# Moving the last tile's second shared step behind the sorted steps of a mixture-of-experts round

## The chip, the cores and the metric

The kernel runs on one core of a Trainium2 chip. The time is device microseconds (us) of one execution. A core has five engines with a queue of instructions each: TensorE (PE in the profile, its weight loads PEld), VectorE (DVE), ScalarE (ACT), GpSimd (POOL) and SyncE (SP). SP issues most of the transfers, POOL the indirect ones. Engines wait for one another and for transfers through semaphores, and each takes its own instructions in order.

## The reference

The input has 4096 rows of 256 numbers. Two layers follow each other. What the change touches is the feed-forward part of the first layer:

```python
for j in range(C):                                   # C = 2 rounds
    residual = xf
    gate = (xf @ router_W[j] + router_b[j]) / TEMP
    _, ids = jax.lax.top_k(gate + gate_bias[j], 2)   # two of 6 experts for each row
    weights = softmax over the two chosen gates
    h  = einsum('nh,ehi->eni', xf, exp_Wup) + exp_bup
    h  = silu(h @ exp_Wg + exp_bg) * h
    eo = h @ exp_Wdown + exp_bdown
    combined = einsum('ne,enh->nh', weights, eo)
    s = (xf @ share_Wup + share_bup).reshape(-1, NS, I)     # NS = 2 shared units
    s = silu(s @ share_Wg + share_bg) * s
    y = residual + combined + (s @ share_Wdown + share_bdown).sum(axis=1)
    xf = y * rsqrt(mean(y * y) + EPS) * norm_w[j]
```

Ahead of it stands an attention part (A below), behind it the second layer's attention (C) and its feed-forward part with 8 experts (D).

## The kernel before

The stages run one after another: A, two expert rounds (B0, B1), C, D. In a round the 4096 rows are 8 tiles (`NB`) of 512 rows. A round is a row of 37 steps (`STEPS`), each of which sends 512 rows through one unit:

- 8 steps "new", numbers 0 to 7: the first shared unit, for tile 0 to 7. They keep their product in `shared` and have no down product of their own.
- 8 steps "old", 8 to 15: the second shared unit for the same tiles. The tile's rows come back from memory (`b_rows`) into one of four slots of `got`. The two shared units have the same down weights, so the product is added to the one kept in `shared` (`joined`, L1539), and one down product serves both. Its result is added to the tile in `x` (L1553).
- 21 steps "sort", 16 to 36, here called s0 to s20: blocks of 512 rows that are sorted by expert. POOL gathers the rows of a block with four indirect transfers into a slot of `got` (`gathers`, L1731), and scatters the results from a slot of `sent` with four more (`scatters`, L1738).

The order of work is written out by hand. `turn_steps` goes through j with three steps at a time: now (j), after (j+1) and third (j+2). PE's body for one j is: gate(after), turn(third), up(after), down(now). The turn is the eight transposes of L1202 of the rows of step j+2; it waits for those rows. Gate and up are 12 matmuls of 512 columns each, down is 24 of 256 columns, and four more in a dense step (L1246). DVE's body is: taken(third), gated(after), send(now). Steps whose unit is new (`fresh`) also have their weights split into a high and a low part, by ACT (L1318) and DVE (L1510).

At the same time the routing is made, spread over the steps. The table by which rows are gathered is summed up in four parts at j = 9 to 12 (`INVERT_AT`, L1694) and turned into the indices `b_gather_i` by `index_vector` (L1699 to L1704) at the end of j = 12. PE's turn at j = 13 waits until the last part has been read from its bank.

POOL's order in a round: wait for the indices (`gather_at`), six gathers (`AHEAD`), then for each k the gather of k+6 and the scatter of k. The first four blocks wait until the dense steps have left `got`, which is the turn of step 15 (in the code: `rnd*STEPS + 2*NB - 1`). A scatter waits for its send (`o`).

At the end of round 0, SP waits for all scatters and fetches, for each tile, its two rows of results per token (`fetch_sync`, into `back`), and ACT (L1419), DVE (L1435, L1437, L1482) and POOL combine and normalise them, tile by tile, before PE can turn tile 0 of round 1. At the end of round 1 the same happens with `close_sync`, whose buffers `close_back` and `x_old` belong to stage C.

Of the kernel before, what the change touches and what calls it, by code (L numbers as in the profile page):

```python
# [14 lines left out]
P = 128  # L15
N, D = 4096, 256
KD = D // P
NT = N // P
TB = 512
NB = N // TB  # L20
# [15 lines left out]
SLOT_TOP = PICKS * N  # L36
CLOSE_BUFS = 4
TURN_COLS = 8
BACKS = 3
# [30 lines left out]
NQ, NGD = max(NQB, NQD), -(-NBD // GROUP)  # L70
STEPS, LB, WM = 2 * NB + NBB, 2 + NBB, KD * D
OUTS = STEPS - NB
# [931 lines left out]
class Round:  # L1004
    def __init__(self, rnd):
        self.rnd, self.first, self.count = rnd, rnd * STEPS, STEPS
        order = [("new", t) for t in range(NB)] + [("old", t) for t in range(NB)] + [("sort", k) for k in range(NBB)]
        self.steps, users = [], {}
        for j, (kind, n) in enumerate(order):
            load = {"new": 0, "old": 1}.get(kind, 2 + n)  # L1010
            i = self.first + j
            self.steps.append(Step(i, kind, rnd * (NBB if kind == "sort" else NB) + n, rnd * LB + load, load not in users, users.get(load - 2)))
            users[load] = self.steps[-1]

    def at(self, j):
        return self.steps[j] if 0 <= j < self.count else None


# [25 lines left out]
def b_sync(sp, b, s, r, d, dram, rnd):  # L1044
    q0, t0, expert = rnd * LB, rnd * NB, {0: slice(0, 1), 1: slice(1, 2)}

    def first_mats(n):
        q = q0 + n
        i, _, previous = RAW_TURN[q]
        if previous is not None:  # L1050
            sp.wait_ge(r.wu_lo.sem, r.wu_lo.at(previous))
        if i >= 2 and n < 2 + RAWS:
            sp.wait_ge(r.joined.sem, r.joined.at(rnd * NB + NB - 1))
        if n >= 2:
            expert[n] = bass.ds(sp.value_load(b.expert_i[0:1, n - 2:n - 1], min_val=NS, max_val=U0 - 1), 1)
        sp.dma_start(b.w_raw[i][:, 0:WM], d["units0"][expert[n], :, 0:WM].squeeze(0)).then_inc(r.loaded[i].sem, 16)
        if q < 2:
            sp.wait_ge(r.folded.sem, r.folded.at(q))
            sp.dma_start(b.w_raw[q][:, WM:2 * WM], b.up_turned[:, q, :]).then_inc(r.loaded[i].sem, 16)
        else:  # L1060
            sp.dma_start(b.w_raw[i][:, WM:2 * WM], dram.folded[expert[n], :, :].squeeze(0)).then_inc(r.loaded[i].sem, 16)
# [23 lines left out]
    if rnd == 1:  # L1085
        for i in range(SENDS):
            sp.wait_ge(r.scattered[i].sem, r.scattered[i].at(uses_of(NBB, SENDS, i) - 1))
        for t in range(BACKS):
            fetch_sync(sp, b, r, dram.kept[0], t)
    for t in range(NB):  # L1090
# [8 lines left out]
    if rnd == 0:  # L1099
        sp.wait_ge(r.fold_kept.sem, r.fold_kept.at(0))  # L1100
    for t in range(NB):
        if t >= 4:
# [5 lines left out]
    for n in range(2, LB + 1):  # L1108
        if n < LB:
            first_mats(n)  # L1110
        if n >= 3:
            last_mat(n - 1)
            biases(n - 1)


def first_sort(kg):
    return (kg // NBB) * STEPS + 2 * NB + kg % NBB


def sort_out(kg):  # L1120
    return (kg // NBB) * OUTS + NB + kg % NBB

# [58 lines left out]
def b_tensor(pe, b, s, r, rnd):  # L1181
# [3 lines left out]
    def turn(st):  # L1185
# [3 lines left out]
        elif st.kind == "old":  # L1189
            t = st.n % NB  # L1190
            pe.wait_ge(r.reloaded[t % 4].sem, r.reloaded[t % 4].at(rnd * 2 + t // 4))
            src = lambda c, f: b.got[:, t % 4, c, f * P:(f + 1) * P]
        else:
# [75 lines left out]

    first, rounds = 2 * NB, (NBB - 2) // TURNS  # L1270
    for j, now, after, third in turn_steps(rnd):
# [32 lines left out]
def b_scalar(act, b, s, r, rnd):  # L1304
    B = b.bank

    def rounded(sig, done, st, lo, hi):
# [6 lines left out]
        elif st.before is not None:  # L1314
            act.wait_ge(done.sem, done.at(index(st.before)))
        elif st.load >= 2:
            act.wait_ge(done.sem, done.at(rnd * (OUTS if done is r.down_ps else STEPS) - 1))
        act.activation(b.w_hi_flat[st.load % 2][:, lo:hi], b.w_raw[i][:, lo:hi], ACT.Copy).then_inc(sig.sem, 1)  # L1318
# [390 lines left out]
def b_gpsimd(g, b, s, r, dram, rnd):  # L1709
# [13 lines left out]
    def gathers(k):  # L1723
# [3 lines left out]
        else:  # L1727
            g.wait_ge(r.gT_ps.sem, r.gT_ps.at(rnd * STEPS + 2 * NB - 1))
        for c in range(QB):
# [49 lines left out]
def close_sync(sp, b, s, r, d, dram):  # L1779
# [9 lines left out]

    old_rows(0)  # L1790
    sp.dma_start(b.heads, d["consts"][:, 1, :]).then_inc(s.load_c_small.sem, 16)
    sp.dma_start(b.c_bo, d["bo_rows"]).then_inc(s.load_c_small.sem, 16)
# [799 lines left out]
def program(nc, d, out):  # L2592
    ctx = ExitStack()
    with ctx:
# [110 lines left out]
        with ExitStack() as sc:  # L2705
# [15 lines left out]
            with ExitStack() as over:  # L2721
                b.sent_both = sb(over, "sent", [P, 2, QB, D])
                b.sent = [b.sent_both[:, i, :, :] for i in range(2)]
                b.back = [b.got[:, 2 * i:2 * i + 2, :, :] for i in range(2)] + [b.sent_both]
                b.junk = sb(over, "junk", [P, 2, D])
# [7 lines left out]
        with ExitStack() as sc:  # L2733
            b.close_back, b.x_old = [sb(sc, f"close_back{t}", [P, PICKS, CT, D]) for t in range(CLOSE_BUFS)], [sb(sc, f"x_old{t}", [P, CT, D]) for t in range(CLOSE_BUFS)]
            b.c_raw = {n: sb(sc, n + "_raw", [P, KD, D]) for n in C_MATS}
# [8 lines left out]
            b.c_outT = sb(sc, "c_outT", [P, KD, TB])  # L2744
            b.c_y, b.c_e, b.c_l, b.c_t = (sb(sc, n, [P, 2 * KD, TB]) for n in ("c_y", "c_e", "c_l", "c_t"))
            bC = Names(b)

# [347 lines left out]
```

## Time and profile before

| | us |
|---|---|
| median of 3 runs | 2036.41 |
| lowest and highest | 2035.42, 2038.35 |
| profiled execution, its own time | 2036.51 |
| its span, first to last instruction | 2034.6 |

| engine | busy us | share of the span |
|---|---|---|
| PE | 1766.5 | 87% |
| PEld | 1559.6 | 77% |
| DVE | 1402.5 | 69% |
| ACT | 1029.3 | 51% |
| POOL | 821.1 | 40% |

The mean granted TensorE clock is 0.927. The profiled execution spent 1.9 us outside its span. A share of the span is an average over stages: what a change is worth is read from the stage that it touches. In the span, round 0 begins at about 658 us, round 1 at about 1045 us, and stage C at about 1426 us.

### The profile page before, as it was taken

The page shows a single profiled execution, that of the slowest core. Times are in us where ns is not written, and L with a number is a line of the kernel's source. Part 1 is how long each engine was busy: PE and PEld are TensorE (multiplying, and loading weights), DVE is VectorE, ACT ScalarE, POOL GpSimd, SP SyncE. Part 2 cuts the span into 40 slices and gives each one's busy share as a digit, 9 for nine tenths or more (in the row PEclk, how much of TensorE's full clock was granted, in tenths as well). Part 3 has the DMA queues.
Part 4 walks back from the last instruction along what each step waited for, and adds up shares of the span by engine and source line. Part 5 has one row for each costly group of instructions (what it writes and reads, how often), then busy time and mean ns, then how long its engine had stood idle before and what let it go on. Part 6 is the DMA issues. An engine that isn't in the chain of part 4 may idle for free. (4 is left out here: it accounts for less than half of the span.)

```text
span 2034.6 us, 31786 instructions
## 1 busy us (share of the span) xinstructions
PE 1766.5 (87%) x11154; PEld 1559.6 (77%) x11154; DVE 1402.5 (69%) x2513; ACT 1029.3 (51%) x2078; POOL 821.1 (40%) x868
## 2 busy tenths in 40 slices
PE   5899999999978999999949999996499883899990
PEld 4788888888877878888838788886266683899990
DVE  4665556546433888777756987775798687688886
ACT  4344334434412344555546355553688353788882
POOL 2132232323211114777721157776221030788840
PEclk8899999999998899999969999998699966899995
DMA  4100000000023131666553226664600013688857
GB/s 155 62 1 11 10 10 0 10 10 0 10 88 103 55 105 40 202 192 202 168 190 122 91 78 199 203 186 146 221 32 1 1 63 114 206 278 277 257 193 258
DMA packets 146216, 231.43 MB, mean 114 GB/s; under 512 B 28082, under 2 KB 103092, under 8 KB 141108
## 3 DMA queue, kind: packets, MB, share of 16 engines
q1 hardware_dynamic: 122484, 165.47, 24.6%
q0 software_dynamic: 23616, 64.52, 10.5%
q8 instruction: 60, 0.98, 0.2%
q14 instruction: 56, 0.46, 0.1%
HBM read 174.07 MB, written 55.33 MB: 113 GB/s over the span
## 5 line engine op out<-in xcount | busy, mean ns | idle before, releaser
L178 POOL TENSOR_TENSOR spare_g<-neg_half 128x1 f32<-128x1 f32 x80 | 20.7, 259 | 622.2 <-ACT a_sg L538 142.5
L167 PE MATMUL bank<-gT_hi,w_hi 128*128 128x512 f32 x592 | 246.0, 416 | 2.4 <-DVE gT_lo L1526 2.4
L167 PE MATMUL bank<-gT_hi,w_lo 128*128 128x512 f32 x592 | 237.3, 401 | 0.0
L167 PE MATMUL bank<-gT_lo,w_hi 128*128 128x512 f32 x592 | 236.2, 399 | 0.0
L1731 POOL DMA_INDIRECT got<-b_rows,b_gather_i x168 | 171.9, 1023 | 65.1 <-issue 50.6
L1526 DVE TENSOR_TENSOR gT_lo<-bank,gT_hi 128x512 fp32r<-128x512 f32 x148 | 97.0, 689 | 132.4 <-ACT gT_hi L1334 99.1
L1364 ACT ACTIVATE m_hi<-gs 128x512 fp32r<-128x512 f32 x116 | 73.0, 633 | 128.3 <-DVE gs L1533 69.0
L167 PEld LDWEIGHTS bank<-gT_hi,w_lo 128*128 128x128 f32 x592 | 113.2, 191 | 27.6
L167 PE MATMUL bank<-w_hi,m_hi 128*128 128x256 f32 x464 | 130.5, 281 | 2.8 <-DVE shared L1555 1.4
L167 PEld LDWEIGHTS bank<-gT_hi,w_hi 128*128 128x128 f32 x592 | 113.6, 192 | 22.9 <-DVE gT_lo L1526 2.5
L167 PEld LDWEIGHTS bank<-gT_lo,w_hi 128*128 128x128 f32 x592 | 113.9, 192 | 21.5
L167 PE MATMUL bank<-w_lo,m_hi 128*128 128x256 f32 x464 | 130.4, 281 | 0.0
L167 PE MATMUL bank<-w_hi,m_lo 128*128 128x256 f32 x464 | 130.1, 280 | 0.0
L2390 POOL DMA_INDIRECT d_got<-d_rows,d_gather_i x78 | 95.7, 1227 | 68.8 <-DVE d_gather_i L2321 45.4
L2396 POOL DMA_INDIRECT d_kept<-d_sent,d_scatter_i x78 | 97.6, 1252 | 45.9 <-DVE d_sent L2551 24.6
L884 POOL TENSOR_TENSOR a_aTm<-a_aT,masks 128x512 f32<-128x512 f32 x56 | 71.4, 1286 | 107.2 <-PE bank L416 82.6
L1355 ACT ACTIVATE gs<-bank,w_cols 128x512 f32<-128x512 f32 x84 | 57.7, 690 | 97.3 <-PE bank L167 97.3
L1738 POOL DMA_INDIRECT b_kept<-sent,b_scatter_i x88 | 90.4, 1028 | 26.8 <-issue 26.8
L167 PE MATMUL bank<-d_gT_hi,v_hi 128*128 128x256 f32 x312 | 93.0, 298 | 1.8 <-DVE d_gT_lo L2531 1.8
L577 ACT ACTIVATE a_ax<-bank 128x512 f32<-128x512 f32 x48 | 28.7, 597 | 128.0 <-PE bank L416 128.0
L1334 ACT ACTIVATE gT_hi<-bank 128x512 fp32r<-128x512 f32 x148 | 82.0, 598 | 21.1 <-PE bank L1202 20.9
L167 PE MATMUL bank<-v_hi,d_m_hi 128*128 128x256 f32 x312 | 91.3, 293 | 1.4 <-issue 0.9
(455 smaller groups left out, 5731.2 us busy)
## 6 DMA issues: line engine op xcount, KB each, us to landing
v_raw<-in_units SPq DMA_DIRECT2D x39, 1024.0 KB, 5.0
w_raw<-in_units SPq DMA_DIRECT2D x52, 256.0 KB, 4.9
shared<-in_units SPq DMA_DIRECT2D x40, 256.0 KB, 4.4
b_rows<-x SPq DMA_DIRECT2D x16, 512.0 KB, 2.9
got<-b_rows SPq DMA_DIRECT2D x16, 512.0 KB, 3.9
close_back<-b_kept SPq DMA_DIRECT2D x16, 512.0 KB, 7.8
d_back<-d_kept SPq DMA_DIRECT2D x16, 512.0 KB, 8.5
w_raw<-b_folded SPq DMA_DIRECT2D x24, 256.0 KB
```

What stands on the lines that cost most here:

```text
L167: ins = pe.matmul(out, a, b, start=first and n == 0, stop=last and n == of - 1)
L178: eng.tensor_tensor(b.spare_g[:, i:i + 1], b.neg_half[:, 0:1], b.neg_half[:, 0:1], ALU.mult)
L577: act.activation(b.ax[:, :], B[1][:, :], ACT.Copy).then_inc(s.ax.sem, 1)
L884: g.tensor_tensor(four(b.aTm[l % 2][:, :]), four(b.aT[:, :]), mid(b.maskT[:, l, :], CT), ALU.mult).then_inc((s.aTm if l else s.aTm0).sem, 1)
L1334: act.activation(b.gT_hi[st.par][:, f, :], B[6 + f][:, :], ACT.Copy).then_inc(r.gT_hi.sem, 1)
L1355: act.activation(product_of(b, st)[:, o, :], B[2 + o][:, :], ACT.Silu, bias=b_bias(b, st, 1, o)).then_inc(r.sg.sem, 1)
L1364: act.activation(b.m_hi[st.par][:, o, :], b.gs[:, o, :], ACT.Copy).then_inc(r.m_hi.sem, 1)
L1526: v.tensor_tensor(b.gT_lo[st.par][:, f, :], B[6 + f][:, :], f32(b.gT_hi[st.par][:, f, :]), ALU.subtract).then_inc(r.gT_lo.sem, 1)
L1731: g.indirect_dma_start(b.got[:, kg % 4, c, :], None, dram.rows[rnd], bass.IndirectOffsetOnAxis(b.gather_i[:, q:q + 1], 0)).then_inc(r.gath ...
L1738: g.indirect_dma_start(dram.kept[rnd], bass.IndirectOffsetOnAxis(b.scatter_i[:, q:q + 1], 0), b.sent[kg % SENDS][:, c, :], None).then_inc( ...
L2390: g.indirect_dma_start(b.got[n % 6][:, c, :], None, rows, bass.IndirectOffsetOnAxis(b.gather_i[:, q:q + 1], 0)).then_inc(r.gathered[n % 6] ...
L2396: g.indirect_dma_start(kept, bass.IndirectOffsetOnAxis(b.scatter_i[:, q:q + 1], 0), b.sent[k % 4][:, c, :], None).then_inc(r.scattered[k % ...
```

## The change

One step of each round is moved: the step "old" of tile 7 leaves place 15 and becomes step 36, behind s20. The sorted steps become 15 to 35. With it:

- The order of steps and all indices that count them (`FRONT_STEPS` = 15). The moved step finds its unit's weights gone, so they are loaded once more (`LATE_LOAD`, one more load in each round, `LB` from 23 to 24) and split again by ACT and DVE.
- SP reloads the last tile's rows at the end of the round's loads, into the slot of `got` that s17 leaves (`row_slot`).
- POOL's first four gathers wait for the turn of step 14 instead of step 15.
- The third and fourth weight buffers (which lie in `shared`) wait for the joined product of tile 6 instead of tile 7.
- `back` is laid out anew: the first fetch goes into `sent_both`, the next two into `got`; the third waits for the turn of the round's last step.
- In stage C the buffers `close_back` and `x_old` are placed elsewhere, with a gap (`C_GAP`) between them, so that the first row of returned data does not touch what the moved step still uses; all further loads of that stage wait for the last send (`o`).

Where the routing is made (j = 7 to 15) does not change.

```diff
+LATE = 1
+FRONT_STEPS, LATE_LOAD = 2 * NB - LATE, 2 + NBB
-STEPS, LB, WM = 2 * NB + NBB, 2 + NBB, KD * D
+STEPS, LB, WM = 2 * NB + NBB, 3 + NBB, KD * D
...
-        order = [("new", t) for t in range(NB)] + [("old", t) for t in range(NB)] + [("sort", k) for k in range(NBB)]
+        order = [("new", t) for t in range(NB)] + [("old", t) for t in range(NB - LATE)]
+        order += [("sort", k) for k in range(NBB)] + [("old", t) for t in range(NB - LATE, NB)]
...
-            load = {"new": 0, "old": 1}.get(kind, 2 + n)
+            load = {"new": 0, "old": 1 if j < FRONT_STEPS else LATE_LOAD}.get(kind, 2 + n)
...
+def row_slot(t, rnd):
+    return t % 4 if t < NB - LATE else (rnd * NBB + NBB + t - (NB - LATE)) % 4
...
         for t in range(BACKS):
+            if t == BACKS - 1:
+                sp.wait_ge(r.gT_ps.sem, r.gT_ps.at(STEPS - 1))
             fetch_sync(sp, b, r, dram.kept[0], t)
...
-    for t in range(NB):
+    for t in range(NB - LATE):
         if t >= 4:
             sp.wait_ge(r.gT_ps.sem, r.gT_ps.at(rnd * STEPS + NB + t - 4))
...
+    for t in range(NB - LATE, NB):
+        sp.wait_ge(r.gT_ps.sem, r.gT_ps.at(first_sort(rnd * NBB + NBB - 4 + t - (NB - LATE))))
+        sp.dma_start(b.got[:, row_slot(t, rnd), :, :], rows_of(dram.rows[rnd], t)).then_inc(r.reloaded[t % 4].sem, 16)
...
         if k >= 4:
             g.wait_ge(r.gT_ps.sem, r.gT_ps.at(first_sort(kg - 4)))
         else:
-            g.wait_ge(r.gT_ps.sem, r.gT_ps.at(rnd * STEPS + 2 * NB - 1))
+            g.wait_ge(r.gT_ps.sem, r.gT_ps.at(rnd * STEPS + FRONT_STEPS - 1))
...
     old_rows(0)
+    sp.wait_ge(r.o.sem, r.o.at(2 * OUTS - 1))
     sp.dma_start(b.heads, d["consts"][:, 1, :]).then_inc(s.load_c_small.sem, 16)
...
-                b.back = [b.got[:, 2 * i:2 * i + 2, :, :] for i in range(2)] + [b.sent_both]
+                b.back = [b.sent_both, b.got[:, 2:4, :, :], b.got[:, 0:2, :, :]]
```

## Rows read from the trace of the kernel before

**Rows 1.** Waits, PE: line, released by, us in total, times, longest.
```profile
PE bank L1202 <- DVE x L1482: 25.8, 1, 25.8
PE bank L2048 <- ACT m_hn L1826: 19.0, 1, 19.0
```
**Rows 2.** Windows: length, busy us of PE PEld DVE ACT POOL, clock, DMA share, GB/s.
```profile
830.00:1000.00 170.00, 170.00 (x1022) 149.25 (x1022) 128.88 (x205) 94.19 (x164) 131.01 (x128) 1.00 0.64 193
1024.20:1045.00 20.80, 0.00 (x0) 0.00 (x0) 7.52 (x15) 8.19 (x28) 4.83 (x8) 0.50 0.54 177
1045.00:1054.90 9.90, 8.58 (x32) 7.51 (x33) 5.74 (x12) 4.96 (x15) 1.47 (x3) 0.50 0.94 302
1734.50:1741.00 6.50, 5.46 (x24) 5.06 (x25) 2.89 (x5) 4.33 (x8) 5.09 (x5) 0.50 0.40 103
```
**Rows 3.** Timeline, POOL, both rounds: start, us, instruction, idle before and releaser.
```profile
804.70 1.22 POOL L1731 DMA_INDIRECT got<-b_rows,b_gather_i  x1 [7.30 <-PE bank L1202]
...
809.20 1.09 POOL L1731 DMA_INDIRECT got<-b_rows,b_gather_i  x1 [0.30 <-issue]
...
1023.60 0.97 POOL L1738 DMA_INDIRECT b_kept<-sent,b_scatter_i  x1 [0.30 <-issue]
...
1195.35 1.09 POOL L1731 DMA_INDIRECT got<-b_rows,b_gather_i  x1 [7.21 <-PE bank L1202]
...
1413.06 0.97 POOL L1738 DMA_INDIRECT b_kept<-sent,b_scatter_i  x1 [0.30 <-issue]
```
**Rows 4.** Timeline, PE, first transposes of steps 15 and s0, both rounds.
```profile
802.71 0.33 PE L1202 MATMUL bank<-ident,got 128*128 128x128 f32 x1
...
812.56 0.38 PE L1202 MATMUL bank<-ident,got 128*128 128x128 f32 x2
...
1193.45 0.33 PE L1202 MATMUL bank<-ident,got 128*128 128x128 f32 x1 [0.16 <-DVE b_found L1694]
...
1203.30 0.27 PE L1202 MATMUL bank<-ident,got 128*128 128x128 f32 x1
```
**Rows 5.** Timeline, DVE, last write of the gather indices, both rounds.
```profile
803.25 0.20 DVE L1704 TENSOR_SCALAR b_gather_i<-b_gather_i 128x84 int32<-128x84 int32 x1
...
1193.98 0.20 DVE L1704 TENSOR_SCALAR b_gather_i<-b_gather_i 128x84 int32<-128x84 int32 x1
```
**Rows 6.** Timeline, stage D, its first gathers: DVE, POOL, PE.
```profile
1726.88 0.20 DVE L2321 TENSOR_SCALAR d_gather_i<-d_gather_i 128x78 int32<-128x78 int32 x1
...
1727.91 1.09 POOL L2390 DMA_INDIRECT d_got<-d_rows,d_gather_i  x1 [45.37 <-DVE d_gather_i L2321]
...
1734.55 0.69 PE L2434 MATMUL bank<-ident,d_got 128*128 128x128 f32 x2 [8.60 <-DMA d_got<-d_rows,d_gather_i]
```
**Rows 7.** Timeline, ACT, first product of the turns of s19 and s20.
```profile
991.15 1.08 ACT L1334 ACTIVATE gT_hi<-bank 128x512 fp32r<-128x512 f32 x2
...
1000.46 1.08 ACT L1334 ACTIVATE gT_hi<-bank 128x512 fp32r<-128x512 f32 x2
```
**Rows 8.** Timeline, DVE, products and sends: a dense step, then both rounds' ends.
```profile
806.72 0.75 DVE L1533 SCALAR_TENSOR_TENSOR gs<-bank,bias_cols,gs 128x512 f32<-128x512 f32 x1 [0.64 <-PE bank L167]
...
809.98 1.28 DVE L1553 TENSOR_TENSOR x<-x,bank 128x512 f32<-128x512 f32 x2
...
1012.04 0.75 DVE L1533 SCALAR_TENSOR_TENSOR gs<-bank,w_cols,gs 128x512 f32<-128x512 f32 x1 [0.65 <-PE bank L167]
...
1014.11 0.68 DVE L1510 TENSOR_TENSOR w_lo<-w_raw,w_hi 128x512 fp32r<-128x512 f32 x1
...
1019.26 0.69 DVE L1555 TENSOR_TENSOR sent<-bank,w_b 128x512 f32<-128x512 f32 x1 [0.66 <-PE bank L167]
...
1402.78 0.75 DVE L1533 SCALAR_TENSOR_TENSOR gs<-bank,w_cols,gs 128x512 f32<-128x512 f32 x1 [0.65 <-PE bank L167]
```
**Rows 9.** Timeline, stage D, the last send and its scatter.
```profile
1987.38 0.69 DVE L2551 TENSOR_TENSOR d_sent<-bank,v_b 128x512 f32<-128x512 f32 x1 [2.72 <-PE bank L167]
...
1988.35 0.97 POOL L2396 DMA_INDIRECT d_kept<-d_sent,d_scatter_i  x1 [1.16 <-DVE d_sent L2551]
```

More of the change, by code:

```diff
@@ L37 @@
 CLOSE_BUFS = 4
+C_GAP = 5168
 TURN_COLS = 8
@@ L1044, in b_sync @@
 def b_sync(sp, b, s, r, d, dram, rnd):
-    q0, t0, expert = rnd * LB, rnd * NB, {0: slice(0, 1), 1: slice(1, 2)}
+    q0, t0, expert = rnd * LB, rnd * NB, {0: slice(0, 1), 1: slice(1, 2), LATE_LOAD: slice(1, 2)}
     def first_mats(n):
@@ L1052, in first_mats @@
         if i >= 2 and n < 2 + RAWS:
-            sp.wait_ge(r.joined.sem, r.joined.at(rnd * NB + NB - 1))
-        if n >= 2:
+            sp.wait_ge(r.joined.sem, r.joined.at(rnd * NB + NB - LATE - 1))
+        if 2 <= n < LATE_LOAD:
             expert[n] = bass.ds(sp.value_load(b.expert_i[0:1, n - 2:n - 1], min_val=NS, max_val=U0 - 1), 1)
@@ L1112, in b_sync @@
             last_mat(n - 1)
-            biases(n - 1)
+            if n - 1 < LATE_LOAD:
+                biases(n - 1)
+    for t in range(NB - LATE, NB):
+        sp.wait_ge(r.gT_ps.sem, r.gT_ps.at(first_sort(rnd * NBB + NBB - 4 + t - (NB - LATE))))
+        sp.dma_start(b.got[:, row_slot(t, rnd), :, :], rows_of(dram.rows[rnd], t)).then_inc(r.reloaded[t % 4].sem, 16)
 def first_sort(kg):
-    return (kg // NBB) * STEPS + 2 * NB + kg % NBB
+    return (kg // NBB) * STEPS + FRONT_STEPS + kg % NBB
 def sort_out(kg):
-    return (kg // NBB) * OUTS + NB + kg % NBB
+    return (kg // NBB) * OUTS + NB - LATE + kg % NBB
 def product_of(b, st):
@@ L1191, in turn @@
             pe.wait_ge(r.reloaded[t % 4].sem, r.reloaded[t % 4].at(rnd * 2 + t // 4))
-            src = lambda c, f: b.got[:, t % 4, c, f * P:(f + 1) * P]
+            src = lambda c, f: b.got[:, row_slot(t, rnd), c, f * P:(f + 1) * P]
         else:
@@ L1268, in step @@
         down(now)
-    first, rounds = 2 * NB, (NBB - 2) // TURNS
+    first, rounds = FRONT_STEPS, (NBB - 2) // TURNS
     for j, now, after, third in turn_steps(rnd):
@@ L1316, in rounded @@
         elif st.load >= 2:
-            act.wait_ge(done.sem, done.at(rnd * (OUTS if done is r.down_ps else STEPS) - 1))
+            ended = LATE if st.load % LB == 0 else 0
+            act.wait_ge(done.sem, done.at(rnd * (OUTS if done is r.down_ps else STEPS) - 1 - ended))
         act.activation(b.w_hi_flat[st.load % 2][:, lo:hi], b.w_raw[i][:, lo:hi], ACT.Copy).then_inc(sig.sem, 1)
@@ L2733, in program @@
         with ExitStack() as sc:
-            b.close_back, b.x_old = [sb(sc, f"close_back{t}", [P, PICKS, CT, D]) for t in range(CLOSE_BUFS)], [sb(sc, f"x_old{t}", [P, CT, D]) for t in range(CLOSE_BUFS)]
             b.c_raw = {n: sb(sc, n + "_raw", [P, KD, D]) for n in C_MATS}
@@ L2745, in program @@
             b.c_y, b.c_e, b.c_l, b.c_t = (sb(sc, n, [P, 2 * KD, TB]) for n in ("c_y", "c_e", "c_l", "c_t"))
+            b.x_old = [sb(sc, f"x_old{t}", [P, CT, D]) for t in range(1, CLOSE_BUFS)]
+            b.c_gap = sb(sc, "c_gap", [P, C_GAP])
+            b.x_old.insert(0, sb(sc, "x_old0", [P, CT, D]))
+            b.close_back = [sb(sc, f"close_back{t}", [P, PICKS, CT, D]) for t in range(CLOSE_BUFS)]
             bC = Names(b)
```

## The prediction

> **What bounds the kernel now.** I read the waits of PE first. The two longest stand where a round hands over: PE waits 25.8 us before it can turn tile 0 of round 1, and 19.0 us at the start of stage C [rows 1]. The change puts one step's PE work into such holes, so the question is what releases PE there and whether that comes sooner. What releases it is the chain scatter, landing, fetch, weigh, mix, square, normalise; it starts with the scatters of the last sorted block s20, which POOL issues.
>
> The windows say how the sorted stretch runs: from 830 to 1000 us PE is busy in all of 170 us at full clock, and POOL for 131 us [rows 2]. The rest of POOL's time is the 0.30 us before each transfer that its timeline puts down to issue. So both are full there. POOL starts its first gather at 804.70 us (1195.35 in round 1) and reaches the first scatter of s20 at 1023.60 (1413.06) [rows 3]; the rows between, 168 transfers to a round, stand back to back. The send of s20 ends at 1019.26 + 0.69 = 1019.95 us [rows 8], 3.65 us before POOL comes to it. So the handover in round 0 is set by POOL, with 3.65 us of slack for PE and DVE, and it moves earlier only if POOL starts earlier, later as soon as the send of s20 comes more than that later.
>
> **Where the sorted stretch can start.** POOL's first gather needs two things, the indices and a free `got`. Now the turn of step 15 is the later one: it starts at 802.71 us [rows 4], and POOL follows at 804.70, released by it [rows 3]. With the change the turn of step 14 is enough, and that is long past; but the indices are written at 803.25 + 0.20 = 803.45 us (1194.18 in round 1) [rows 5], and the change leaves their place alone. In stage D, POOL's first gather starts 1727.91 - 1727.08 = 0.83 us after the indices [rows 6]. So the gathers start at 804.28 instead of 804.70, and at 1195.01 instead of 1195.35. POOL gains 0.42 and 0.34 us, not a step.
>
> PE's side is what the change does turn over. At j = 13 PE's order is gate(14), turn of the third step, up(14), down(13). That third step was the dense one, whose rows had been in `got` for long; now it is s0, whose gathers have not begun. In stage D the same row of events, four gathers and a turn that waits for them, takes 1734.55 - 1727.91 = 6.64 us [rows 6]. So PE turns s0 at 804.28 + 6.64 = 810.92 us in round 0, and at 1201.65 in round 1. Before, it turned s0 at 812.56 and 1203.30 [rows 4]. The whole step that was taken out of the front comes back as a stall: PE stands from 802.71 to 810.92 us (8.2 us) and from 1193.29 to 1201.65 us (8.4 us), and the sorted steps gain 1.64 and 1.65 us. Behind the waiting turn stand up(14), down(13) and the rest of PE's queue; DVE and ACT wait for these, and have nothing else in that stretch.
>
> The four gathers took 809.20 - 804.70 = 4.50 us from first to fourth start in round 0 [rows 3]. The Trainium skill (SBUF — State Buffer, section "Who interferes with whom") says that a DVE instruction with two SBUF inputs contends with a GpSimd instruction that reads SBUF. By that rule DVE, which stands still while PE stalls, leaves these gathers alone; by round 0's row they stay slow and the first turn is some 0.6 us later. Independently of that, I take stage D's 6.64 us, whose gathers ran in the same situation (PE waiting for them), and keep the longer interval for the range.
>
> **The clock.** PE runs at half clock (1.2 GHz) in the windows that follow its long waits. While it waits for round 1 the clock falls to 0.50 and stays there for 9.9 us after PE has work again; in stage D, after the wait of 8.60 us, it is 0.50 in the 6.5 us from PE's restart on [rows 2, 6]. A stall of 8.2 or 8.4 us in a stretch that ran at full clock is new. I expect the clock to fall in it and to stay down for about 6.4 us of dense work, which takes twice as long: 3.2 us lost in each round, all of it, since PE is full behind the stall. The bounds are nothing (clock kept) and half of 9.9, which is 4.95 us. I take 3.2 because the stage D row is the one with a wait of the same length and dense matmuls behind it.
>
> **The end of a round.** One step takes 1000.46 - 991.15 = 9.31 us [rows 7]. Up to now nothing follows s20: its up is followed by down(s19) and at once by down(s20). With the change, the order is gate(s20), turn(36), up(s20), down(s19), then gate(36) and up(36) of the dense step, and only then down(s20). DVE's order also puts the dense step's product, its joining, its low part and its down weights ahead of send(s20). Step by step for round 0:
>
> - the second half of the product of s20 starts at 1012.04 us [rows 8]; that of step 36 starts one step later, 1021.35;
> - in a dense step the send is complete 809.98 + 1.28 - 806.72 = 4.54 us after that start [rows 8]; the fresh down weights put another 0.60 us ahead of it (row at 1014.11, from which the next one starts 0.60 us later);
> - that is 1026.49 us for the send of s20; less 1.64 for the earlier turn of s0, plus 3.2 for the clock: 1028.05;
> - from a send to the scatter it releases 1988.35 - 1988.07 = 0.28 us [rows 9]: 1028.33 us, against 1023.60: 4.7 us later.
>
> In round 1 the product starts at 1402.78 us: 1402.78 + 9.31 + 4.54 + 0.60 - 1.65 + 3.2 + 0.28 = 1419.06, against 1413.06 [rows 3, 8]: 6.0 us later. There the slack was smaller. POOL now waits for the send, so its 0.42 and 0.34 us are worth nothing.
>
> **What the moved step does in the hole.** Its down product waits for the send of s20 (same bank) and takes, by its share of a dense step's columns (28 x 256 of 20480) and the 9.85 us of that step [rows 4], an estimated 3.4 us; with its own send it is done 4.1 us after the send of s20. The four scatters, at 0.97 + 0.30 us each, take 3.8 us from first to last start, and their landing more; so step 36 is done before SP gets past the scatters, and it delays nothing. The waits added for `back` (turn of step 36) and in `close_sync` (last `o`) are met by then and cost nothing; if the last send came late, the loads of the stage C matrices would queue behind it on SP, with the 19 us wait of PE as cover [rows 1]. PE's hole shrinks by the step that fills it. That is not time won: the handover is released by the scatters, and some 18 us of hole remain (from 1028.05 + 3.4 = 1031.5 to 1045.0 + 4.7 = 1049.7), after which I expect the clock to be down as before [rows 2].
>
> **Small parts, all hidden.** The third load of the shared unit is 3 transfers of 256 KB per round on SP, which waits for weight buffers most of the time; its splitting is 3 ACT and 3 DVE instructions in a place where every sorted step has the same six, so PE's pace stays. The tile's reload can be issued when s17's slot is free, four turns (37 us) before PE needs it, less what SP still waits for. `back` and stage C in new places move the same bytes; I give them nothing, within 0.5 us either way.
>
> **Sum.** 4.7 + 6.0 = 10.7 us on the profiled execution's own 2036.51 us: 2047.2 us. That execution lies 0.1 us from the median of the runs shown.
>
> **Rivals.**
>
> *The clock holds.* The stall in front does not pull the clock down. For it: PE is fully busy before and after. Against: both long waits read here have half clock behind them [rows 2, 6]. Then 10.7 - 6.4 = 4.3 us: 2040.8 us.
>
> *The clock stays down longer*, as at the start of round 1 (9.9 us), and the gathers take round 0's 4.50 us: 10.7 + 2 x 1.75 + 0.6 = 14.8 us: 2051.3 us. For it: the turn and the dependent steps behind it do not fill PE at once.
>
> *Not slower: the step in the hole keeps the clock up.* The place is the handover of round 0. If short stalls leave the clock alone, then PE's idle time there, shortened by the 9.8 us between the two turns in rows 4, may too. The price is the half clock at the start of round 1, 9.9 / 2 = 4.95 us. With the front's clock held as well: 4.3 - 4.95 = -0.65, 2035.9 us. It decides from the point where an idle stretch of 18 us leaves the clock at full; the 20.8 us window at 0.50 speaks against it.
>
> *Not slower or faster: s0's rows are there in time.* If the sorted steps really ran a step earlier, the send of s20 would be no bound (1026.5 - 9.8 = 1016.7 us) and POOL alone would set the end: 0.42 + 0.34 us won, 2035.7 us; if POOL's start moved by a step too, up to 12 us. Rows 5 are against it: the indices are not there.
>
> **Chances.** The forecast with its clock loss 0.60; clock holds 0.13; longer 0.13; not slower by the first 0.07, by the second 0.07. The likeliest case alone spans 2044 to 2051 us. The range reaches down to 2037.5, which takes in the clock that holds, and up to 2052.5, which takes in the longer one; what remains outside is most of the last two cases and a little above. About 0.2% (4.1 us) is what a measurement can tell from no change. Slower by more than that: the forecast, the longer case and half of the case in which the clock holds, 0.80. Within it: 0.15. Faster: 0.05.
>
> **What would show it.** In the changed trace: PE's transposes of s0 waiting about 8 us for `got<-b_rows`, in both rounds; a clock of 0.5 right behind; the first gathers at about 804.3 and 1195.0; POOL's last four scatters no longer back to back with the ones before but released by DVE's send; that send about 8 us later than 1019.95; PE's wait for L1482 at about 18 us instead of 25.8. It is wrong if PE does not wait at s0, if the clock is full behind the wait, or if the sends of s20 still come before POOL is free.

## The result, and the profile after

Over five runs of each, the changed kernel takes 2047.13 us in the median (2046.60 to 2048.96) and the kernel before 2037.39 us (2035.42 to 2038.83): ratio 1.0045, 95% interval 1.003 to 1.006, so 6 to 12 us slower. The profiled execution took 2047.13 us, with a span of 2045.3 us against 2034.6 before. The forecast was 2047.2 us, slower with a chance of 0.80. It was built on 2036.51 us, as 10.7 us more; against the five runs before the difference is 9.7.

The waits of PE in the changed kernel (line, released by, us in total, times, longest) have a new entry. The first row answers to the 25.8 us of [rows 1], the second was not there before:

```profile
PE bank L1217 <- DVE x L1498: 16.6, 1, 16.6
PE bank L1217 <- issue: 16.5, 2, 8.3
```

The hole between the rounds became shorter, because step 36 lies in it, and two stalls of 8.2 and 8.3 us came in at the front. Their releaser is given as "issue", that is, none that the profile shows; what PE stood for is told by the instruction behind the stall. These are the timeline rows of PE and POOL, in round 0 and then in round 1:

```profile
813.09 1.94 PE L1217 MATMUL bank<-ident,got 128*128 128x128 f32 x8 [8.31 <-issue]
...
805.93 1.56 POOL L1747 DMA_INDIRECT got<-b_rows,b_gather_i  x1 [6.35 <-DVE b_gather_i L1720]
807.80 0.95 POOL L1747 DMA_INDIRECT got<-b_rows,b_gather_i  x1 [0.30 <-issue]
809.05 0.95 POOL L1747 DMA_INDIRECT got<-b_rows,b_gather_i  x1 [0.30 <-issue]
810.30 0.94 POOL L1747 DMA_INDIRECT got<-b_rows,b_gather_i  x1 [0.30 <-issue]
...
1206.23 1.94 PE L1217 MATMUL bank<-ident,got 128*128 128x128 f32 x8 [8.18 <-issue]
...
1199.18 1.45 POOL L1747 DMA_INDIRECT got<-b_rows,b_gather_i  x1 [6.33 <-DVE b_gather_i L1720]
```

The first gather is now released by the write of the indices (L1720), not by PE as in [rows 3], and PE's transposes read what the four gathers bring. The indices themselves did not move; this row of DVE answers to [rows 5]:

```profile
805.44 0.20 DVE L1720 TENSOR_SCALAR b_gather_i<-b_gather_i 128x84 int32<-128x84 int32 x1
```

From the end of this write to POOL's start it is 805.93 - 805.64 = 0.29 us; 0.83 was forecast. DVE is not idle when this gather starts; two writes later it has

```profile
805.72 0.68 DVE L1526 TENSOR_TENSOR w_lo<-w_raw,w_hi 128x512 fp32r<-128x512 f32 x1
```

Windows around the stall (length, busy us of PE, PEld, DVE, ACT and POOL, clock, DMA share, GB/s) show the clock:

```profile
802.00:807.00 5.00, 2.78 (x12) 1.88 (x11) 4.23 (x12) 2.58 (x5) 1.07 (x1) 1.00 0.00 0
807.00:810.00 3.00, 0.00 (x0) 0.00 (x0) 0.00 (x0) 0.00 (x0) 2.39 (x3) 0.50 0.30 86
810.00:813.10 3.10, 0.01 (x1) 0.04 (x1) 0.00 (x0) 0.00 (x0) 2.19 (x3) 0.50 0.28 86
813.10:817.20 4.10, 4.10 (x14) 3.62 (x15) 1.98 (x3) 1.71 (x3) 3.19 (x4) 0.50 0.38 114
817.20:822.00 4.80, 4.80 (x35) 4.49 (x35) 3.67 (x6) 1.63 (x3) 3.64 (x4) 1.00 0.30 94
```

The clock falls to 0.50 (1.2 GHz) at 807.0 us, 2.2 us into the stall, and stays there for 4.1 us after PE has work again, with PE busy in all of it; before, the same stretch ran at 1.00. In round 1 it is the same for 3.5 us.

The end of the round, POOL first. The first row is the first scatter of s19, the second the last one, the third the first of s20, and the fourth the first of s20 in round 1. The last two answer to 1023.60 and 1413.06 of [rows 3]:

```profile
1019.63 0.97 POOL L1754 DMA_INDIRECT b_kept<-shared,b_scatter_i  x1 [1.24 <-DVE shared L1571]
...
1023.46 0.97 POOL L1754 DMA_INDIRECT b_kept<-shared,b_scatter_i  x1 [0.30 <-issue]
1029.26 0.97 POOL L1754 DMA_INDIRECT b_kept<-sent,b_scatter_i  x1 [4.83 <-DVE sent L1571]
...
1422.12 0.97 POOL L1754 DMA_INDIRECT b_kept<-sent,b_scatter_i  x1 [4.83 <-DVE sent L1571]
```

POOL, which before came to s20's scatters without a gap, now stands 4.83 us for the send in both rounds. And DVE, where the product, joining, low part and down weights of the dense step stand ahead of that send (the first three as in front of 809.98 in [rows 8]):

```profile
1023.84 0.75 DVE L1549 SCALAR_TENSOR_TENSOR gs<-bank,bias_cols,gs 128x512 f32<-128x512 f32 x1 [0.65 <-PE bank L170]
1024.51 1.29 DVE L1555 TENSOR_TENSOR gs<-gs,shared 128x512 f32<-128x512 f32 x2
1025.89 1.30 DVE L1558 TENSOR_TENSOR m_lo<-gs,m_hi 128x512 fp32r<-128x512 f32 x2
1027.10 0.69 DVE L1526 TENSOR_TENSOR w_lo<-w_raw,w_hi 128x512 fp32r<-128x512 f32 x1
1027.70 1.28 DVE L1571 TENSOR_TENSOR sent<-bank,w_b 128x512 f32<-128x512 f32 x2
```

The hole itself, PE's first row of step 36's down product and the turn of round 1's tile 0:

```profile
1029.13 0.55 PE L170 MATMUL bank<-w_hi,m_hi 128*128 128x256 f32 x1 [2.58 <-DVE sent L1571]
...
1050.67 1.97 PE L1217 MATMUL bank<-ident,x 128*128 128x128 f32 x8 [16.61 <-DVE x L1498]
```

From s20's first scatter to this turn it is 1050.67 - 1029.26 = 21.41 us; before it was 1045.02 - 1023.60 = 21.42. The moved step cost the handover nothing, as forecast.

**Where the 10.7 us of the two spans lie.** Take the start of the last write of `b_hot_id` by POOL in each round as the point from which to count (792.98 and 1183.71 us before, 795.17 and 1188.43 after), since nothing ahead of it in the round depends on the edit. Then the sum closes: +2.19 us up to it in round 0, +3.47 from it to s20's first scatter, -0.01 over the handover, -0.93 from tile 0's turn to the same write of round 1, +4.34 to s20's scatter there, +1.64 from there to the end of the span; together +10.70. The two terms of the change's own places are 3.47 + 4.34 = 7.8 us. The other 2.9 net lie where its steps don't reach.

The first turn of round 0 comes at 658.0 to 660.6 us in the twelve profiles of this case, whose kernels share the code up to it. It comes after 660 us in just four of them (the changed kernel, filled, three_before and fetch_first), and these four are the ones that show the clock at 0.50 for 3.4 us at 595 to 600, where the eight others are at full clock: that goes with +2.19. That this one stretch at half clock makes them late is likely, but no run tested it. The stretch from s20's first scatter of round 1 to the end is 621.6 us in the one profile of the kernel before, but 624.4 in early_gather and 623.4 in three_before, which keep the old places of the buffers; the changed kernel's 623.2 is no sign of a cost.

Five runs of each give 6 to 12 us and can't tell 7.8 from 10.7. In the series of the experiments the kernel before had medians of 2039.6 (35 runs), 2039.8 (29) and 2040.0 us (21), so its 2037.4 here may be a low draw; 2047.1 is 7.5 above 2039.6. The changed kernel was not run again in these series.

### The profile page after: what moved, and what is told of

Read it like the earlier page. It is cut to its first block and busy times, and to the rows that moved or that the text cites. A ratio compares the mean times of both kernels' runs of the same rounds, so it can differ in the third digit from the quotient of the medians.

```text
span 2045.3 us, 31812 instructions
## 1 busy us (share of the span) xinstructions
PE 1775.0 (87%) x11154; PEld 1568.5 (77%) x11154; DVE 1407.3 (69%) x2519; ACT 1031.7 (50%) x2084; POOL 819.0 (40%) x868
## 5 line engine op out<-in xcount | busy, mean ns | idle before, releaser
L170 PEld LDWEIGHTS bank<-w_hi,m_hi 128*128 128x128 f32 x464 | 89.1, 192 | 8.0 <-issue 5.5
L1754 POOL DMA_INDIRECT b_kept<-shared,b_scatter_i x80 | 82.9, 1036 | 25.3 <-issue 24.1
```

The lines of the kernel that those rows point to most:

```text
L170: ins = pe.matmul(out, a, b, start=first and n == 0, stop=last and n == of - 1)
L1754: g.indirect_dma_start(dram.kept[rnd], bass.IndirectOffsetOnAxis(b.scatter_i[:, q:q + 1], 0), b.sent[kg % SENDS][:, c, :], None).then_inc( ...
```

## The experiments

Ratios are to the kernel before, run beside each on the same chip, with 95% intervals. A difference to the changed kernel is taken over its own ratio, 1.0045, which adds some 3 us of uncertainty, and may be some 2 us too large for the reason just given. Where a profile is compared, it is one execution of each kernel, counted from `b_hot_id`.

**send_first** (changed kernel; PE and DVE finish s20 before the dense step's gate, up and product):

```diff
         if j == STEPS - 2:      # PE's loop, ahead of gate(after)
+            down(now)
-        if now is not None and now.out is not None:
+        if now is not None and now.out is not None and j != STEPS - 2:
             down(now)
 ...                             # DVE's loop: the same with send(now)
```

> The changed kernel, but at the last sorted step PE runs down(s20) and DVE send(s20) ahead of the dense step's gate, up and product. The changed kernel has 2047.1 us (2037.4 before). Theory: the handover is released by the scatters of s20, and in the changed kernel these wait for the send that stands behind the dense step; POOL itself would be free 4.5 us (round 0) and 5.2 us (round 1) earlier. So the scatters of s20 are back to back with those before, and the time falls by some 9.7 us to 2037.5. Rival: PE's stall in front and its clock set the time, and whatever PE does last it is late by them: then the time stays at 2045 to 2047.

Ratio 1.0009 (1.0000 to 1.0018), profiled span 2041.1 us: 7.3 us back of the 9.7 expected. Its POOL rows, the last scatter of s19 and the first of s20:

```profile
1022.08 0.97 POOL L1758 DMA_INDIRECT b_kept<-shared,b_scatter_i  x1 [0.30 <-issue]
1023.35 0.97 POOL L1758 DMA_INDIRECT b_kept<-sent,b_scatter_i  x1 [0.30 <-issue]
```

Back to back again, so the dense step's place ahead of the send was what POOL had waited for: from `b_hot_id` to s20's scatter it is 229.9 and 229.5 us, against 234.1 and 233.7. But the handover grew from 21.4 to 1047.47 - 1023.35 = 24.1 us, and here is why. PE's down product of step 36 and SP's queue:

```profile
1030.96 0.35 PE L170 MATMUL bank<-w_hi,m_hi 128*128 128x256 f32 x1 [4.15 <-DVE m_lo L1560]
```

```profile
1030.89 0.33 SPq L1077 DMA_DIRECT2D w_raw<-in_units  x1
1031.39 0.93 SPq L1147 DMA_DIRECT2D sent<-b_kept  x2
```

Step 36 is now the late one. A load of round 1's weights stands ahead of the fetches on SP and waits for step 36 to free its buffer, and the fetches follow only at 1031.39. The last scatter was issued at 1027.17 us; in the changed kernel SP's fetch comes 2.4 us after the last issue (1033.09 to 1035.52), which would be 1029.6. So 1.8 of the 2.7 us are lost on SP; the other 0.9 lie between the fetch and ACT's first use of its rows (6.3 us against 5.4).

The end of round 1 costs more, which the expectation left out. The loads of stage C wait for the last `o`, which is step 36's:

```profile
1426.53 0.35 SPq L1812 DMA_DIRECT2D heads<-in_consts  x1
```

That is 12.9 us after s20's first scatter (1413.68); in the changed kernel it was 7.8. From this scatter to the end of the span it is 627.4 us, against 623.2. So the profile gives 8.3 us back up to the two scatters and takes 2.7 and 4.2 behind them, which leaves 1.4; its whole span is 4.2 us shorter, the rest lies in stretches that the edit doesn't reach. The 7.3 us of the ratio are more than the profile accounts for.

**turn_late** (changed kernel; only PE's order at j = 13: up(14) and down(13) ahead of s0's turn):

```diff
-            turn(third)
+            if j != FRONT_STEPS - 2:
+                turn(third)
         ...                     # up(after), down(now)
+        if j == FRONT_STEPS - 2:
+            turn(third)
```

> The changed kernel, but at j = 13 PE runs up(14) and down(13) ahead of the turn of s0 that waits for the gathers. Theory: 6 us of the 8.3 us stall are filled, some 2.4 us come back as a wait for the split rows of s0, so the sorted steps run about 3.7 us earlier, or up to 5.7 with the clock kept; the send of s20 is then near the point where POOL is free (4.5 and 5.2 us earlier than now), and the time falls by 7 to 9.5 us, to 2038 to 2040. Rival, that the order at the end of the round is the whole cost: the time stays at 2046 to 2047.

Ratio 1.0001 (0.9992 to 1.0009), span 2038.7: 9.0 us back by two lines of order. The work that had been queued behind the stall now fills it. PE, s0's turn and the first matmul behind it:

```profile
810.99 1.09 PE L1217 MATMUL bank<-ident,got 128*128 128x128 f32 x8 [1.89 <-DMA got<-b_rows,b_gather_i]
...
813.66 0.80 PE L170 MATMUL bank<-gT_hi,w_hi 128*128 128x512 f32 x1 [1.57 <-DVE gT_lo L1545]
```

From s0's turn to the end of s20's send it is 212.6 and 212.4 us instead of 215.9 and 215.6. That is 3.3 us less a round, 6.5 in all up to s20's scatters; the runs' 9.0 have 3 us of uncertainty and don't contradict it. POOL still waits 1.86 us for the send of s20, so the late order at the end still costs something. A full clock is not what it brought: the waits are only 1.89 and 1.57 us, but the clock is at 0.50 from 812.4 to 819.2 us, as this window from behind them shows:

```profile
817.00:819.00 2.00, 2.00 (x7) 1.42 (x6) 2.00 (x4) 1.48 (x3) 1.45 (x2) 0.50 0.48 94
```

**both** (the two edits together).

> Both edits of the two kernels beside it, at the front and at the end of each round. Theory: POOL is the bound once the send of s20 is in time, so the two gains don't add: the same as the better one alone, 2037 to 2038. Rival, that PE's queue sets the handover: both gains add, some 2030.

Ratio 0.9996 (0.9987 to 1.0005), span 2038.1. From `b_hot_id` to s20's scatter it is 229.1 and 229.7 us, with scatters back to back:

```profile
1021.25 0.97 POOL L1761 DMA_INDIRECT b_kept<-shared,b_scatter_i  x1 [0.30 <-issue]
1022.53 0.97 POOL L1761 DMA_INDIRECT b_kept<-sent,b_scatter_i  x1 [0.30 <-issue]
```

s20's send is complete at 1018.23, 4.3 us before POOL comes to it. Alone the edits gave 7.3 and 9.0 us, together 10.0, so they don't add. Up to s20's scatters POOL's queue is the bound again, and what PE wins past it is slack. Behind them this kernel pays as send_first does: its handover takes 21.9 us, and from s20's scatter of round 1 to the end it is 627.5 us, against 623.2. So POOL alone does not explain where the gain stops.

**filled** (changed kernel; 32 extra matmuls of 512 columns while PE would stand at s0; nothing reads what they write):

```diff
+            if j == FRONT_STEPS - 2:
+                for n in range(FILL):     # FILL = 32
+                    pe.matmul(B[7][:, :], part(after, 1, n % KD, 0, P)[0],
+                              b.gT_hi[after.par][:, n % KD, :], start=True, stop=True)
             turn(third)
```

> The changed kernel with 32 extra matmuls of 512 columns (about 7.5 us) in PE's queue ahead of the turn of s0, written into a bank that the turn overwrites, so nothing that is computed changes. PE's stall becomes work, the order stays. Theory: the clock stays at full, where the changed kernel runs 4.1 us (round 0) and 3.5 us (round 1) at half clock behind the stall; half of that, 2.05 + 1.75 = 3.8 us, is won: 2043.3. Rival, that the clock costs nothing because something else is waited for there: 2047. Rival, that the extra matmuls delay the turn: above 2047.

Ratio 1.0023 (1.0014 to 1.0032): 4.5 us back. Windows over its stall and behind its restart:

```profile
807.00:810.00 3.00, 3.00 (x14) 2.43 (x13) 0.00 (x0) 0.00 (x0) 2.39 (x3) 1.00 0.25 75
...
813.20:817.30 4.10, 4.10 (x24) 3.56 (x25) 2.63 (x5) 1.60 (x3) 3.19 (x4) 1.00 0.38 109
```

24 matmuls in the 4.1 us in which the changed kernel did 14, at full clock. With useless work in the hole the turn comes no sooner (7.1 us after the first gather in both), so this isolates the clock's part. The first interval from turn to turn (s0 to s1) measures it per round: 9.80 and 9.79 us before, 11.74 and 11.48 changed, 9.85 in both rounds here. The clock costs 1.9 and 1.6 us a round, 3.5 in all; the runs' 4.5 agree within their uncertainty.

Not all of it reaches the end of the round. Counted from `b_hot_id`, s20's scatters come 1.6 us earlier in round 1, but only 0.8 in round 0, because PE there comes to s19's rows before they have landed:

```profile
1001.46 0.77 PE L1218 MATMUL bank<-ident,got 128*128 128x128 f32 x5 [0.93 <-DMA got<-b_rows,b_gather_i]
```

**early_gather** (kernel before; each of the first four groups of gathers waits only for the step that holds its own `got` slot, not for the last one of the front):

```diff
-            g.wait_ge(r.gT_ps.sem, r.gT_ps.at(rnd * STEPS + 2 * NB - 1))
+            g.wait_ge(r.gT_ps.sem, r.gT_ps.at(rnd * STEPS + 2 * NB - 4 + kg % 4))
```

> The kernel before, with one edit: each of POOL's first four gathers waits only for the dense step that holds its own slot of got (steps 12 to 15), not all for step 15. PE's order is untouched. Theory: POOL starts when the indices are there, 0.9 us earlier in each round as in the changed kernel, is full from there on, and releases both handovers 0.9 us earlier: 1.8 us less than the kernel before, ratio 0.999. Rival, that POOL doesn't bound the handover: no difference at all, 1.000.

Ratio 0.9988 (0.9976 to 0.9999), median 2035.78 against 2039.75, span 2036.0. It has the part of the change that wins and none that costs. POOL's first gather:

```profile
803.78 1.22 POOL L1731 DMA_INDIRECT got<-b_rows,b_gather_i  x1 [6.34 <-DVE b_gather_i L1704]
```

Counted from `b_hot_id`, the gathers start 0.95 and 0.89 us earlier and s20's scatters 1.3 us in round 0, 0.05 in round 1. POOL has no other wait in round 1 either; its transfers themselves took 0.8 us more there (168.6 against 167.7 us, summed). This is the only complete kernel here whose interval lies below one, and only just; its profile accounts for 1.3 of the 2.4 us that the ratio gives.

**three_before** and **three_after** (the two kernels with three of the four gathers of each sorted block; the fourth quarter of the rows is left out, so POOL has 21 transfers fewer a round):

```diff
+            if c == QB - 1:
+                continue
             g.indirect_dma_start(b.got[:, kg % 4, c, :], None, ...)
```

> The kernel before, but each sorted block gathers three of its four parts (the fourth part of the slot keeps what lay there, so the expert results are not the reference's). POOL has 21 transfers less in each round, some 27 us. Theory: POOL then no longer sets the handover; the send of s20 does, 3.4 us (round 0) and 2.1 us (round 1) before the point where POOL now comes to it: 5.5 us less, ratio 0.9973, and not 54 us less. Rival, that PE alone bounds the stretch already: 1.000. Rival, that POOL's whole time counts: 0.974.

> The changed kernel with the same edit (three of four parts gathered, results not the reference's). Theory: in the changed kernel POOL waits for the send of s20, so its freed time is worth nothing there; what is won is that the rows of s0 are there one gather earlier, 1.25 us in each round, so 2.5 us less than the changed kernel: ratio 1.0033 (1.0045 before the edit). Rival, that POOL bounds it as before: 5 us or more less, 1.002 or below.

Ratios 0.9990 (0.9982 to 0.9999) and 1.0048 (1.0036 to 1.0061). The second missed what I expected (1.0033): with a quarter of POOL's gathers gone the changed kernel is not measurably faster. Its profile does show s0's turn 1.3 and 1.2 us earlier from `b_hot_id`, and s20's scatters 1.8 and 0.9; the five runs can't show that much. What POOL waits for is as in the changed kernel, so it is the send that sets the end, not POOL's work:

```profile
1025.83 0.97 POOL L1756 DMA_INDIRECT b_kept<-sent,b_scatter_i  x1 [4.84 <-DVE sent L1571]
```

The first gave about half of what I expected or less: 2.0 us by the ratio, 2.9 up to s20's scatters in the profile, of 5.5. POOL's rows of three_before, first and last scatter of s19 and first of s20:

```profile
1018.72 0.97 POOL L1740 DMA_INDIRECT b_kept<-shared,b_scatter_i  x1 [3.64 <-DVE shared L1555]
...
1022.53 1.31 POOL L1740 DMA_INDIRECT b_kept<-shared,b_scatter_i  x1 [0.30 <-issue]
1024.15 0.97 POOL L1740 DMA_INDIRECT b_kept<-sent,b_scatter_i  x1 [0.30 <-issue]
```

With POOL idle for 3.64 us before s19's send, s20's scatters still stand back to back behind s19's four. So a POOL that is ahead of time gains only until the scatters of s19 wait for their own send: from `b_hot_id` 1.9 us in round 0 and 1.0 in round 1. Of the 3.65 us by which s20's send was ahead of POOL before, 1.75 are left.

**layout_only** (kernel before with the new places of `back`, `close_back` and `x_old` and the added wait for the last `o`, without the moved step):

```diff
+    sp.wait_ge(r.o.sem, r.o.at(2 * OUTS - 1))
-                b.back = [b.got[:, 2 * i:2 * i + 2, :, :] for i in range(2)] + [b.sent_both]
+                b.back = [b.sent_both, b.got[:, 2:4, :, :], b.got[:, 0:2, :, :]]
 ...                             # close_back and x_old behind stage C's tiles
```

> The kernel before with only the new places of back, close_back and x_old, and the wait for the last o in stage C's loads; the dense step stays in its place. Theory: the buffers' places cost nothing, 1.000. Rival: the 1.6 us that the changed kernel loses between the second handover and its end come from the new places: 1.0008.

Ratio 0.9996 (0.9987 to 1.0006): the buffers cost nothing that can be measured. The rival, 1.6 us at the end (1.0008), lies just outside the interval; the 623.4 and 624.4 us of the old layout, above, speak against it too.

**fetch_first** (send_first; in round 1 the load that held SP is issued behind the first three fetches):

```diff
         first_mats(n)
-        last_mat(n)
+        if n == 0 or rnd == 0:
+            last_mat(n)
 ...                             # behind the fetches of the round
+        last_mat(1)
```

> The kernel that sends s20 first (ratio 1.0009), with one more edit: in round 1, SP issues the down weights of the second shared unit behind the first three fetches of returned rows. Without the edit SP stood until 1030.89 us at that load, which waits until the moved step has split its own weights, and the fetches were behind it (1031.39). Theory: the handover of round 0 takes 21.5 us again from the last block's first scatter to PE's turn, instead of 24.1: 2.6 us less, ratio 0.9996. Rival, that the moved step's work on ACT and DVE delays the handover: no change, 1.0009.

Ratio 1.0008 (0.9998 to 1.0018). The fetch is no longer held by the load:

```profile
1031.46 0.93 SPq L1149 DMA_DIRECT2D sent<-b_kept  x2
```

It comes 6.25 us after s20's first scatter at 1025.21; in the changed kernel it was 6.26, in send_first 8.04. Yet the handover took 23.5 us, not 21.5. So SP's queue was the cause of the late fetch, and it was not the whole cause of the longer handover: with both fetches at the same distance, 2.1 us remain between fetch and turn. DVE's rows tell what holds them, the last send of step 36, the low parts of the weights, and only then the weighing of the fetched rows:

```profile
1037.94 0.69 DVE L1573 TENSOR_TENSOR x<-x,bank 128x512 f32<-128x512 f32 x1 [0.98 <-PE bank L1263]
1038.55 1.28 DVE L1530 TENSOR_TENSOR w_lo<-w_raw,w_hi 128x512 fp32r<-128x512 f32 x2
1039.75 1.66 DVE L1455 SCALAR_TENSOR_TENSOR sent<-sent,r_gb 128x256 f32<-128x256 f32 x4
```

ACT takes up the fetched rows 5.5 us after the fetch, as in the changed kernel (5.4). DVE does so after 8.3 us, against 6.0 there, 2.3 us later. The trace shows this; no run moved DVE's work to test it.

**index_early** (fetch_first; the tables behind the gather indices a step earlier, INVERT_AT = NB):

```diff
-ROUTE_AT, COUNT_AT, INVERT_AT, GATES_AT = NB - 2, NB - 1, NB + 1, NB + 5
+ROUTE_AT, COUNT_AT, INVERT_AT, GATES_AT = NB - 2, NB - 1, NB, NB + 5
 ...                             # ACT's hot_part(0) at the end of its j
```

> The kernel beside it, and the four parts of the gather table are summed up one step earlier (j = 8 to 11), so the indices are there one step earlier and s0's rows can be in place when PE comes to them. Theory: the stall of 8.3 us in front of s0 goes, with its 2 us of clock, but a stall of some 6.5 us opens at j = 8, where PE waits for the first part of the table that DVE and POOL make, with some 2 us of clock; sorted steps some 1.8 us earlier in each round: 3.6 us less than the kernel beside it, 0.998. Rival, that early indices make the move pay in full: some 12 us less than before in each pair of rounds, 0.994. Rival, that nothing is won because POOL bounds: the same as beside it.

Ratio 1.0008 (0.9998 to 1.0017), where 0.998 was expected: the same as fetch_first. s0's rows are now in time and PE doesn't stall there, but it stalls where the tables are read:

```profile
764.71 1.56 PE L1278 MATMUL bank<-b_hot_id,b_hot_in 128*128 128x168 bf16 x10 [8.18 <-POOL b_hot_id L1745]
```

8.18 us at j = 8, with the half clock behind it. Counted from round 0's first turn (658.99 us here, 660.49 in fetch_first), the indices are complete only 1.4 us earlier, not a step. And they no longer release the first gather; PE does, whose turn of step 14 came late by the stall:

```profile
805.80 1.22 POOL L1755 DMA_INDIRECT got<-b_rows,b_gather_i  x1 [8.80 <-PE bank L1219]
```

From the same point this gather starts 1.0 us later than in fetch_first, s0's turn comes 1.7 us later, and s20's first scatter at the same distance (364.7 us). The step that the change took out of the front is waited for somewhere: with the tables early at their first reading, otherwise at s0.

## Why the prediction was right

**PE's stall at s0: right.** 8.3 and 8.2 us against 8.2 and 8.4. The gathers started 10.76 us after `b_hot_id` in place of 11.72, so POOL gained 0.96 and 0.89 us where 0.42 and 0.34 stood in the sum: the 0.83 us from index to gather, taken from stage D, is 0.29 here. It changed nothing, since the four gathers and their landing took longer than the 6.64 us of [rows 6] (7.16 and 7.05 us): s0's turn is 1.66 and 1.79 us earlier net of the drift, against 1.64 and 1.65. Two errors cancelled. The Trainium skill (SBUF — State Buffer, section "Who interferes with whom") says that a DVE instruction with two SBUF inputs contends with a GpSimd instruction that reads SBUF. With DVE idle in the stall the second to fourth gathers took 0.95, 0.95 and 0.94 us. The first took 1.56 and 1.45 us, and beside it DVE was not idle, as the prediction had it: it started inside `w_lo<-w_raw,w_hi`, two inputs from SBUF. So both agree with the rule.

**The clock: mechanism right, the term too large.** The step of the sum that failed is "I expect the clock to fall in it and to stay down for about 6.4 us of dense work": it fell, and stayed down for 4.1 and 3.5 us. The loss was 1.9 and 1.6 us (turn to turn), not 3.2 in each round. The wait of 8.60 us in stage D was as long as these; its length alone did not set how long the clock stayed down. Nor did the place: behind that wait of stage D (8.5 to 8.7 us in ten profiles) the clock stayed down for 6.0 to 8.5 us, and behind the stall at s0 for 2.9 to 4.9 us in the four kernels that keep it (the changed one, send_first, three_after, fetch_first). The 6.4 us were one draw from another place. The rival in which the clock holds is out by these windows and by filled. The one in which it stays down longer is out by the 4.1 and 3.5 us. The one in which the step in the hole keeps it up is out as well: the clock is at 0.50 from 1039.1 us, and for 12.3 us behind the turn of tile 0, against 9.9 before. And s0's rows were not there in time.

**The order at the end: right.** From s0's turn to the end of s20's send it took 215.90 and 215.62 us, before 207.39 and 207.38: 8.51 and 8.24 more. Less the clock's 1.9 and 1.6 that is 6.6 us in both rounds for the dense step's place ahead of the send, against 1026.49 - 1019.95 = 6.54. (With a full clock in filled, 6.6 us remain in round 1 and 7.8 in round 0, where PE waits for s19's rows: a cost that the sum does not have.) Then the send releases POOL after 0.27 us. In sum -1.66 + 8.51 + 0.27 - 3.65 = 3.47 us in round 0 and -1.79 + 8.24 + 0.27 - 2.38 = 4.34 in round 1, against 4.7 and 6.0: 7.8 us where 10.7 was forecast, and all but 0.1 of the difference is the clock's term. That the median still lies at the forecast is luck in that part: 2.9 us of the profile's difference come from stretches that the sum took as unchanged, and they make up for the clock's term.

**The handover and the small parts: right.** 21.41 us against 21.42, and layout_only within 0.1%. The hole left was 16.6 us, not some 18: step 36's down product took 4.9 us, not 3.4, with the clock at 0.50 from 1028.8 to 1032.2. The cover that I named for the added wait and for SP's queue is thinner than "step 36 is done before SP gets past the scatters" says: as soon as the send of s20 comes first, step 36 is the late one and SP waits for it. One count is off, without effect: between POOL's first gather and s20's first scatter stand 164 transfers; 168 takes in s20's own four.

**Still open.** Why the stretch behind s20's scatter of round 1 is 627.2 to 628.9 us in the four kernels that send s20 first and 621.6 to 624.4 in the eight others; in one of the four, the run called both, SP's loads of stage C come only 1.3 us later than in the changed kernel, so the wait for `o` alone is not shown to be the cause. And what sets how long the clock stays down.

## What to carry to other kernels

A step taken out from in front of a dependent chain doesn't shorten the chain: ask first what releases the chain's head (here the indices), and count the time to the next work as a stall if that doesn't move. When an engine executes in order and must wait, put everything that is ready in front of the wait, not behind it; and of two pieces at the end of a phase, the one that others wait for goes first; then follow the other one too, which has become the late one (2.7 and 4.2 us here). A slack read off one queue holds only to the next item in that queue that has its own release.

## What was not expected of the hardware

- After stalls of 8.3 and 8.2 us inside a stretch that ran at full clock, the granted clock stayed at 0.50 for only 4.1 and 3.5 us, against 6.5 in stage D and 9.9 at round 1's start [rows 2]. And waits of only 1.89 and 1.57 us with 1.1 us of work between them, in turn_late, were followed by half clock as well.
- POOL's transfers take longer when they start inside a DVE instruction whose two inputs both come from outside the matmul banks. In the two rounds of the kernel before (790 to 1430 us) 109 of 336 do, and take 1.14 us in the mean, up to 1.46; the others take 0.97. Who starts first decides: the 123 transfers during which such a DVE instruction starts take 0.97 us too, none above 1.01. The same two instructions met in both rounds, DVE first in round 0 and POOL first in round 1:

```profile
807.39 1.28 DVE L1539 TENSOR_TENSOR gs<-gs,shared 128x512 f32<-128x512 f32 x2
807.48 1.41 POOL L1731 DMA_INDIRECT got<-b_rows,b_gather_i  x1 [0.31 <-issue]
...
1198.00 0.95 POOL L1731 DMA_INDIRECT got<-b_rows,b_gather_i  x1 [0.30 <-issue]
1198.12 1.28 DVE L1539 TENSOR_TENSOR gs<-gs,shared 128x512 f32<-128x512 f32 x2
```

- In the rounds an indirect transfer that follows a DVE write started 0.27 to 0.29 us after the write's end on POOL, for gathers as for scatters, where stage D had shown 0.83.
- Profiles of kernels with the same code ahead of a point differ by up to 2.6 us at that point, and here the late ones are those with one more 3.4 us at half clock on the way. A difference of a few us between spans has to be counted from a point inside.
